# Four graph layers on one core: the products after layers two and three take 128 rows of the table of sums instead of 64, with 64 rows of zeros

## What is computed

```python
# layer two
neigh = segment_sum(feat[edge_src], edge_dst)
h = (1.0 + eps[0]) * feat + neigh
h = maximum(h @ W1 + b1, 0.0) @ W2 + b2        # W1: 64 x 128, W2: 128 x 64
x = x + h
# layer three
agg = segment_sum(x[src], dst); mean = agg / maximum(cnt, 1.0)
out = relu(mean @ W_l.T + b_l + x @ W_r.T)      # W_l: 64 x 64
```

## Time and profile before

| | us |
|---|---|
| median of 3 executions | 10077.51 (10077.34 to 10081.64) |
| the profiled execution, its own time | 10058.88 |
| its span, first to last instruction | 10057.1 |
| mean granted TensorE clock | 0.623 |

### The profile page before, as it was taken

The page is one execution under the profiler, slowest core; times in us unless marked ns, Lnnn a source line. Parts: engine busy times, 40 slices in busy tenths (PEclk is TensorE's granted clock), DMA queues, the critical chain, the costliest instruction groups (busy, mean ns, idle before and its releaser), DMA issues. The chain is left out here.

```text
span 10057.1 us, 125440 instructions
## 1 busy us (share of the span) xinstructions
PE 5680.5 (56%) x34164; PEld 5281.3 (53%) x34165; DVE 3254.1 (32%) x4806; ACT 635.1 (6%) x1574; POOL 7470.8 (74%) x6820
## 2 busy tenths in 40 slices
PE   5666666666656488888888533333333533333334
PEld 5565555556556488888888533333333433333334
DVE  9433333333333443333333411111111311111112
ACT  3000000000000100000000200000000100000000
POOL 0788888888888677777777677777777477777776
PEclk6555555555555677777777756565565565656555
DMA  2333333333333522222222111111111111111111
GB/s 69 27 20 20 20 20 20 20 20 20 20 20 20 85 45 43 43 43 43 43 43 43 27 27 27 27 27 27 27 27 25 28 27 27 27 27 27 27 27 34
DMA packets 685045, 310.44 MB, mean 31 GB/s; under 512 B 593664, under 2 KB 597610, under 8 KB 684602
## 3 DMA queue, kind: packets, MB, share of 16 engines
q0 software_dynamic: 399360, 218.53, 18.6%
q1 hardware_dynamic: 284183, 90.59, 3.9%
q10 hardware_dynamic: 1444, 0.62, 0.0%
HBM read 223.89 MB, written 85.35 MB: 31 GB/s over the span
## 5 line engine op out<-in xcount | busy, mean ns | idle before, releaser
L938 POOL DMA_INDIRECT h_rows<-h_tab,idx x3328 | 3163.8, 951 | 1155.6 <-issue 943.1
L738 POOL DMA_INDIRECT parts_tab<-total,row_at x1664 | 2563.8, 1541 | 702.5 <-issue 504.3
L1490 PE MATMUL ps_seg<-hot,h_rows 128*64 128x128 f32 x6656 | 1496.3, 418 | 2572.3 <-DMA h_rows<-h_tab,idx 2494.9
L1490 PEld LDWEIGHTS ps_seg<-hot,h_rows 128*64 128x64 f32 x6656 | 1354.3, 226 | 2701.6 <-issue 1935.7
L938 POOL DMA_INDIRECT a_rows<-a_tab,idx x1664 | 1582.1, 951 | 547.3 <-issue 506.5
L1419 DVE TENSOR_TENSOR acc_t<-acc_t,ps_seg 64x128 f32 x416 | 116.4, 280 | 2891.0 <-PE ps_seg L1490 2891.0
L1110 PE MATMUL ps_seg<-hot,act_rows 128*65 128x128 f32 x3328 | 658.2, 380 | 309.2 <-ACT act_rows L1183 308.8
L650 PE MATMUL ps_dst<-identb,relb 128*128 128x128 bf16 x1672 | 216.3, 310 | 1085.0 <-DVE relb L586 1085.0
L1110 PEld LDWEIGHTS ps_seg<-hot,act_rows 128*65 128x65 f32 x3328 | 589.7, 203 | 332.9 <-issue 327.2
L650 PEld LDWEIGHTS ps_dst<-identb,relb 128*128 128x128 bf16 x1672 | 161.4, 141 | 1121.0 <-DVE relb L586 1119.8
L666 PE MATMUL ps_tot<-msg,same 128*128 128x64 f32 x3328 | 649.6, 377 | 98.4 <-issue 98.4
(11 more groups left out here) (184 smaller groups left out, 5910.0 us busy)
## 6 DMA issues: line engine op xcount, KB each, us to landing
h_rows<-h_tab,idx POOLq DMA_INDIRECT x3328
edge<-edge_t SPq DMA_DIRECT2D x208, 132.0 KB
parts_tab<-total,row_at POOLq DMA_INDIRECT x1664, 3.1
a_rows<-a_tab,idx POOLq DMA_INDIRECT x1664
parts_tab<-acc_t SPq DMA_DIRECT2D x3, 3360.0 KB
idx<-src_steps SPq DMA_DIRECT2D x624, 4.0 KB, 1.5
u_win<-u_tab SPq DMA_DIRECT2D x208, 32.0 KB
b_win<-b_tab SPq DMA_DIRECT2D x208, 32.0 KB, 2.2
```

The source lines that it names most:

```text
L738: pool.indirect_dma_start(parts_tab[:, :], bass.IndirectOffsetOnAxis(ap=row_at[:, b, k:k + 1], axis=0), total[:, b, k, :], None, compute_o ...
L938: pool.indirect_dma_start(dest[:, r, k, :], None, table[:, :], bass.IndirectOffsetOnAxis(ap=idx[:, r, k:k + 1], axis=0)).then_inc(landed[r ...
L1490: last = pe.matmul(ps_seg[0:F, b, 0, :], rows_of[:, r, k, :], hot[:, b, k, :], start=(k == 0), stop=(k == K - 1))
```

## The change

`w21_sb` and `wl3_sb` get 128 partitions, and their inputs are padded by 64 rows of zeros. Both products read all 128 partitions of `acc_t`, and the clearing before each edge stage takes all 128 partitions, so that the upper half holds zeros. Order, buffers and counts of instructions stay as they were on every engine; only the shapes of the two products, of the clearing and of two weight transfers change.

```diff
-        w21_sb = sb(ctx, "w21_sb", [F, HID])
+        w21_sb = sb(ctx, "w21_sb", [P, HID])
...
-        wl3_sb = sb(ctx, "wl3_sb", [F, F])
+        wl3_sb = sb(ctx, "wl3_sb", [P, F])
...
-                        dve.memset(acc_t[0:F, :], 0.0).then_inc(cleared, 1)
+                        dve.memset(acc_t[:, :], 0.0).then_inc(cleared, 1)
...
-                        pe.matmul(ps_hid[:, g % HB, :], w21_sb[:, :], acc_t[0:F, g * GN:(g + 1) * GN], start=True,
+                        pe.matmul(ps_hid[:, g % HB, :], w21_sb[:, :], acc_t[:, g * GN:(g + 1) * GN], start=True,
                                   stop=True).then_inc(hid_done, 1)
...
-                            last = pe.matmul(ps_l[:, g % 4, q, :], acc_t[0:F, j * P:(j + 1) * P], wl3_sb[:, :],
+                            last = pe.matmul(ps_l[:, g % 4, q, :], acc_t[:, j * P:(j + 1) * P], wl3_sb[:, :],
                                              start=True, stop=True)
...
-        "w21": v["L2_gnn_W1"],
+        "w21": np.concatenate([v["L2_gnn_W1"], f32((F, HID))], 0),
...
-        "wl3": v["L3_gnn_W_l"].T,
+        "wl3": np.concatenate([v["L3_gnn_W_l"].T, f32((F, F))], 0),
```

## The result

| | before | after |
|---|---|---|
| median of 6 executions, us | 10078.24 (10076.58 to 10083.68) | 10040.33 (10022.17 to 10044.58) |
| the profiled execution, its own time | 10058.88 | 10022.17 |
| its span | 10057.1 | 10020.4 |
| node stage of layer two, first product to last addition | 98.6 | 60.5 |
| last stage, first of its products to last addition | 47.8 | 47.8 |

The ratio is 0.9960, with a 95% interval from 0.9949 to 0.9970: 38 us faster. The two stage lengths are worked out in each trace, from the start of the first L1522 (L1599) to the end of the last L1559 (L1608).

A forecast was written before the change was run, and what follows sets the result against it. TensorE was taken to set both node stages, layer two's mostly at half clock. That stage falls from 98.2 to 61.3 us, gain 36.9, say 37.2 with the drains; 10077.5 - 37.2 = 10040.3 us, range 10030 to 10067.

The forecast's parts named there:

- The drains: Layer two's node stage: changes between 64-row and 128-row products empty TensorE, 0.48 us a group; removing them gains 11.7 us.
- The prediction's argument against the waits: Layer one's loads carry semaphore waits too, without such a gap, so the 0.48 us a group are not semaphore waits.
- The clock rises with six tall passes in a row: Start of layer two's stage: six full-height passes of 512 columns bring the clock to 1.00 after at most some 5 us.
- the term of 1 us for the start: Layer two's stage: half a us or more lost before the clock's first rise, entered in the sum as 1 us.
- Groups of 1.79 us: Layer two's stage at full clock: a hidden pair of 2 x 0.427 us plus eight output passes of 0.94 us.
- The waits: Layer two's stage: TensorE waits for `hid` while ScalarE squares a quarter, 3.3, 2.8 and 2.7 us, 8.8 in all.
- The clock comes back: Layer two's stage: after each wait for `hid` full clock returns, each loss costing some 2.5 us; chance 0.43.
- the third loss: Layer two's stage: the clock's loss after the third wait falls at the stage's end and was left out of the sum.
- The rival: Layer two's stage: clock lost at the first wait and not back; stage 72.3 us, gain 25.9, time 10051.6; chance 0.30.
- The sum: Layer two's stage: 46.5 groups, 8.8 waits, 5.0 clock losses, 1 start, 61.3 us against 98.2; gain 36.9, say 37.2.
- The last stage, the clearing, the weights: Last stage bound by loads at half clock, clearing timed by columns, weight transfers covered: each taken as 0 us.
- last stage too: Last stage also at full clock, groups of 1.87 instead of 3.42 us: 20.2 us more gain, time 10020.1; chance 0.06.

The follow-up runs named there:

- run with 65 rows: The changed kernel with layer two's hidden products at 65 rows and the last stage back at 64; layer two's stage 89.4 us, ratio 0.9996 to the kernel before.
- only layer two at 128: The changed kernel with the last stage's products back at 64 rows; layer two's stage 62.6 us, ratio 0.9968 to the kernel before.
- the changed kernel again: The changed kernel run once more, unaltered, on a chip with 10059.01 us for the kernel before; median 10022.48 us, ratio 0.9965.
- later squares with three more: The changed kernel with ScalarE's squares later, quarters shifted, and three unused 512-column products before the last stage; median 9994.63 us, ratio 0.9936 to the kernel before.
- 96 rows: The changed kernel with layer two's hidden products at 96 rows and the last stage back at 64; layer two's stage 71.4 us, ratio 0.9993 to the kernel before.
- later squares: The changed kernel with ScalarE squaring four groups after a quarter's end instead of two, quarters ending at 8, 14, 20; layer two's stage 49.7 us, ratio 0.9945.

## Why the prediction held

*The drains.* Forecast 0.48 us a group and 11.7 us in all, though 24 x 0.48 is 11.5. The run with 65 rows shows both: 3.42 us a group, 11.5 us of the stage. The prediction's argument against the waits, does not carry it, since the products of those rows lie inside a group and have no wait; this run does. What the traces show of the emptying that the prediction assumed is the outputs' first weight load: 0.86 us ahead of its pass at 65 rows, and only with it at 64.

*The clock rises with six tall passes in a row.* Forecast at most some 5 us after the start, an estimate that no row gives. In the profiled execution it stood at 1.00 before the first product, by luck of where the edge stage ended, so the term of 1 us for the start came out at 0. In three other traces with 128 rows (only layer two at 128, the changed kernel again, later squares with three more) it stood at 0.50 and rose after 6.1, 6.2 and 6.0 us. So the rise is shown for 128 rows, against 64 and 65 that never rose (100.9 and 89.4 us at 0.50), and the delay was forecast 1 us short.

*Groups of 1.79 us* came out at 1.75: the eight output passes took 0.84 us (7811.44 - 7810.60) where 0.94 was taken from the earlier trace rows, and the hidden pair 0.91 us (7812.35 - 7811.44) where it was 0.85. The row of 1.87 us runs to the end of its last load and is no price of a pass in this mixture.

*The waits* of 3.3, 2.8 and 2.7 us came out at 3.35, 2.60 and 2.77, and ScalarE's square was their cause: with it moved, 1.9 us are left of 8.7.

*The clock comes back.* This was the open step, given 0.43 against 0.30. It came back both times, each 3.4 us after it fell, at a cost of 1.7 us each, where I had 2.5. In three other traces there was one loss of 6.8 us, after the first wait, in place of the first two short ones. The prediction put the third loss at nothing, since it falls at the stage's end; the last 16 output passes ran at half clock and took 3.55 us, some 1.8 us more than at full. The rival was a near one: at 96 rows it is what happens. I had argued the return from layer one's stage alone, where the products are other ones; the runs show that it hangs on the height of the long passes, which nothing in the trace of before could show. That the forecast's branch and not the rival came true was therefore a guess that held.

*The sum.* The prediction takes 7889.20 for the last addition; that is where the last product ends, and the addition ends at 7889.66. By its own measure, to the last product, 61.3 us were forecast for the stage and 60.1 measured. The terms: groups 45.5 (46.5 forecast), waits 8.7 (8.8), two losses 3.4 (5.0), start 0 (1), third loss 1.8 (nothing); some 0.7 us are left over. The gain was forecast at 36.9, then 37.2, and is 38.1 in the stage and 36.7 in the span (the stage began 1.1 us later after the change, and what lies between it and the last stage took 0.2 us more). The forecast of 10040.3 meets the median of 10040.33 more closely than the argument deserves, and that is luck: its parts are off by 1 to 2 us in both directions, and the executions timed run from 10022 to 10045.

*The last stage, the clearing, the weights* at 0: the last stage took 47.8 us as before, and the clearing 11.15 us on 128 partitions:

```profile
L1399 DVE MEMSET acc_t<- x2: 11152/11152/11152, 5694.9 to 7871.8; 128x13312 f32 x2
```

The under 1 us for the weights without their cover was an estimate; no run takes the cover away.

*The rival "last stage too"* supposed that the edge stage can leave the clock high just as the products begin, and that taller products then hold it. The first happened in two traces with 128 rows there (later squares, the changed kernel again); the second did not, the clock fell after 1.6 and 1.9 us. After three or four wide products the same stage held it. So the rival was right that the stage can hold full clock, and wrong that the edge stage's remainder is enough.

## What to carry to other kernels

Look at the granted clock of a stage whose TensorE is never idle. If it is at half, ask how many rows the products feed. Zeros in the unused rows cost nothing in time here (a hidden pair at half clock takes 1.82 us at 65 rows and at 128); they brought the mean clock of layer two's stage from 0.51 to 0.91, and ended the 0.48 us a group between products of 64 and of 128 rows. Once the clock was up, the waits that had been covered at half speed were bare, 8.7 us in all, and most cost the clock too, for 3.4 us or more, so the next gain was in the order of the engine that they wait for. The last stage, which held full clock at 128 rows but did not raise it, was worth four wide products ahead of it: they took 5.2 us and gained 13.9 net.

## What was not expected of the hardware

- Holding full clock needed less than raising it: at 96 rows the clock held for 26 us of mixed products and never came back in 44 us of the same mixture without a wait, and the last stage's thin products at 128 rows held it for 26 us behind wide ones but sat at 0.50 for 44.4 us where they started there. Found at 1.00 right after a rest of 1.6 us, they lost it within 2 us.
- The kernel before took 14% longer on one chip than on two others. The edge stages have a part in it (layer two's 2,465 us in the run with 65 rows against 2,097 in the kernel before), while the last stage took the same 47.8 us. Why was not tried and stays open.
